# Macaron block (FFN, Mamba, FFN): other slots for the last two full iterations and an earlier preparation of the next group

## What is computed

```
x = x + 0.5 * ffn(layernorm(x))          # mixture of 8 experts, top 2, hidden 176 each, plus a shared FFN of 352
x = x + mamba(layernorm(x))              # 256 inner channels, 16 states, convolution of 4 taps, selective scan
x = x + 0.5 * ffn(layernorm(x))          # the same weights as the first
```

## Time and profile before

| what | value |
|---|---|
| median of 3 runs | 1891.11 us (1890.74 to 1896.28) |
| profiled execution, own time | 1897.91 us |
| span of its trace | 1896.2 us |
| mean granted TensorE clock in it | 0.956 |
| busy: PE, DVE, POOL, ACT | 1672.0, 1543.4, 1435.9, 1230.4 us |
| scans of iterations 12, 14, 15 begin at | 1404.26, 1618.79, 1713.01 us |
| last scan begins at | 1799.6 us |

### The profile page before, as it was taken

How to read it: one execution, slowest core, us unless ns; L and a number is a source line. 1 busy time by engine, 2 the same in 40 slices (tenths; PEclk the granted TensorE clock), 3 DMA queues, 4 the chain that set the end, 5 groups by cost and what they waited for, 6 DMA issues and landing times.

```text
span 1896.2 us, 27794 instructions
## 1 busy us (share of the span) xinstructions
PE 1672.0 (88%) x7378; PEld 1004.6 (53%) x7378; DVE 1543.4 (81%) x2337; ACT 1230.4 (65%) x1838; POOL 1435.9 (76%) x1318
## 2 busy tenths in 40 slices
PE   5888788989899998989989998999989898957488
PEld 3454444556565555556555555655555555634255
DVE  1358989899888988989888988989888998988732
ACT  2367677676858676676767676676766767665421
POOL 3346878878888887888888888788878888877753
PEclk9998799999999999999999999999999999979698
DMA  5127667686867778586777767677676868767742
GB/s 157 42 73 169 154 163 193 146 188 158 193 166 173 177 168 188 142 194 167 179 169 166 184 156 185 171 173 183 155 191 148 193 152 192 169 143 188 158 104 67
DMA packets 121344, 305.11 MB, mean 161 GB/s; under 512 B 19300, under 2 KB 40519, under 8 KB 106823
## 3 DMA queue, kind: packets, MB, share of 16 engines
q0 software_dynamic: 18432, 125.84, 33.5%
q1 hardware_dynamic: 98406, 174.46, 32.6%
q10 hardware_dynamic: 4320, 2.71, 0.5%
HBM read 167.67 MB, written 5.24 MB: 91 GB/s over the span
## 4 chain that ended last, share of the span: by engine, by line
PE 34%; DVE 19%; issue 15%; POOL 15%; ACT 8%; DMA 7%; DVEq 1%; ACTq 0%; SPq 0%; POOLq 0%
PE ps_y L1101 9%; DVE hist L927 7%; POOL prod L628 6%; PE ps_h2b L1109 5%; POOL gated L568 5%; PE ps_h1a L1087 5%; PE ps_h1b L1087 4%; DMA yacc<-prod 4%; PE ps_h2a L1109 3%; DVE ps_db L879 3%; DVE gated L907 2%; PE ps_m L1048 2%; ACT decay L691 2%; PE ps_m L1152 2%; DVE yacc L996 1%
## 5 line engine op out<-in xcount | busy, mean ns | idle before, releaser
L628 POOL TENSOR_TENSOR prod<-hist,crow 128x1024 f32<-128x1024 f32 x224 | 556.4, 2484 | 232.1 <-DVE hist L927 227.4
L1101 PEld LDWEIGHTS ps_y<-down_w,gated 128*128 128x128 f32 (+1 forms) x3584 | 471.8, 195 | 287.3 <-issue 156.2
L927 DVE TENSOR_TENSOR_SCAN hist<-decay,ps_db 128x1024 f32<-128x1024 f32 x256 | 583.2, 2278 | 2.8
L568 POOL TENSOR_TENSOR gated<-gated,silu 128x512 f32<-128x512 f32 x352 | 492.3, 1455 | 79.7 <-DVE gated L907 71.2
L1101 PE MATMUL ps_y<-down_w,gated 128*128 128x128 f32 (+1 forms) x3584 | 489.2, 281 | 68.2 <-POOL gated L568 67.1
L879 DVE TENSOR_TENSOR ps_db<-du,ps_db 128x1024 f32<-128x1024 f32 x256 | 313.0, 1222 | 103.9 <-PE ps_db L1069 101.2
L691 ACT ACTIVATE decay<-delta,a_neg 128x510 f32<-128x510 f32 x512 | 326.8, 708 | 5.7 <-DVE delta L970 4.3
L711 ACT ACTIVATE silu<-ps_h1a 128x512 f32<-128x512 f32 (+1 forms) x224 | 133.1, 594 | 257.2 <-PE ps_h1a L1087 256.5
L1087 PE MATMUL ps_h1a<-xnT,up_w 128*128 128x512 f32 (+1 forms) x448 | 238.7, 614 | 10.7 <-issue 10.7
L1087 PE MATMUL ps_h1b<-xnT,up_w 128*128 128x512 f32 x448 | 238.9, 615 | 5.2 <-ACT silu L711 4.7
L1109 PE MATMUL ps_h2b<-xnT,up_w 128*128 128x512 f32 x448 | 237.2, 612 | 1.7 <-DVE gated L907 1.7
(11 more groups left out here) (139 smaller groups left out, 1946.4 us busy)
## 6 DMA issues: line engine op xcount, KB each, us to landing
yacc<-prod POOLq DMA_DIRECT2D x112, 1024.0 KB, 10.0
crow<-c_rows SPq DMA_DIRECT2D x128, 512.0 KB, 5.0
wrow<-w_rows SPq DMA_DIRECT2D x320, 128.0 KB, 6.4
wrow<-w_rows SPq DMA_DIRECT2D x64, 224.0 KB, 7.0
wrow<-w_rows SPq DMA_DIRECT2D x64, 192.0 KB, 4.5
wrow<-w_rows SPq DMA_DIRECT2D x64, 160.0 KB, 3.0
yacc<-yacc POOLq DMA_DIRECT2D x16, 512.0 KB, 7.7
wrow<-w_rows SPq DMA_DIRECT2D x64, 96.0 KB, 3.2
```

Source lines behind the costliest of these rows:

```text
L568: nc.gpsimd.tensor_tensor(gated[:, pos % NGATE, :], gated[:, pos % NGATE, :], silu[:, (pos + NCHUNK * f_parity(of, f)) % NSILU, :], ALU.mu ...
L628: nc.gpsimd.tensor_tensor(prod[:, (pair - 1 + odd) % 2, s % 2, :, :], hist[:, s % 2, :, :], c_all, ALU.mult).then_inc(prod_done, 1)
L927: nc.vector.tensor_tensor_scan(hist[:, s % 2, :, :].rearrange("p h t -> p (h t)"), decay[:, s % NA, :, :, :].rearrange("p h b t -> p (h b ...
L1101: ins = nc.tensor.matmul(ps_y[:, t * C:(t + 1) * C], gated[0:rd, posd % NGATE, t * P:(t + 1) * P], down_w[0:rd, jd, :], start=(posd == 0 a ...
```

## The change

For iterations 14 and 15 there are tables of their own: END_UNIT puts the 14 chunks of the second FFN in slots 0, 2, 4 to 26, END_PLAN puts addy1 in slot 31 instead of 21, and END_SP has the row loads at later slots and store_x in slot 31, behind store_w1 and w1:0 to w1:3. Because chunks of the second FFN are now still read after slot 23, where xT1 writes the input of the next ones, xT1 writes xnT[0] in iterations 14 and 16 and xnT[1] in 15 (`second`); xnT[0] is free there.

In PLAN, which holds for the middle iterations and from which START_PLAN and END_PLAN are derived, dt0 and dt1 move from slots 17 and 18 to 14 and 15, sp_exp and xproj from 20 to 16, bparts from 22 to 16, sp_ln from 22 to 18, delta from 26 to 20, du from 28 to 22; in2 and in3 move from 14 and 15 to 19 and 21, wT0 from 16 to 17. The unit of slot 15 moves to 16. On SP store_w0 and w0:0 to w0:3 stand together in slot 18 (before 17 to 19).

```diff
@@ -54,20 +54,20 @@
     PLAN = {
         0: ["stats0"], 1: ["scale0"], 2: ["norm0"], 3: ["addy0", "fold"], 4: ["xT0"], 5: ["stats2", "scale2", "logits0"],
         6: ["norm2", "rcopy0"], 7: ["gate_y0", "xT2"], 8: ["gate_y1", "in0a"], 9: ["in0"], 10: ["outproj"],
-        11: ["resid", "route0"], 12: ["stats3", "in1a", "tilt0"], 13: ["in1", "scale3"], 14: ["in2", "ln_norm", "weights0"],
-        15: ["in3", "ln_scale"], 16: ["wT0", "ln_shift"], 17: ["dt0"], 18: ["dt1", "ln_add"], 19: ["stats1"],
-        20: ["sp_exp", "xproj", "scale1"], 21: ["addy1"], 22: ["norm1", "sp_ln", "bparts"], 23: ["xT1"], 24: ["logits1"],
-        25: ["rcopy1", "route1"], 26: ["cT", "delta"], 27: ["bT", "tilt1"], 28: ["weights1", "du"], 30: ["wT1"],
+        11: ["resid", "route0"], 12: ["stats3", "in1a", "tilt0"], 13: ["in1", "scale3"], 14: ["dt0", "ln_norm", "weights0"],
+        15: ["dt1", "ln_scale"], 16: ["sp_exp", "xproj", "bparts", "ln_shift"], 17: ["wT0"], 18: ["sp_ln", "ln_add"],
+        19: ["in2", "stats1"], 20: ["delta", "scale1"], 21: ["addy1", "in3"], 22: ["norm1", "du"], 23: ["xT1"],
+        24: ["logits1"], 25: ["rcopy1", "route1"], 26: ["cT"], 27: ["bT", "tilt1"], 28: ["weights1"], 30: ["wT1"],
     }
     EARLY = ("addy0", "addy1", "resid")
 
-    UNIT = {s: (1, pos) for pos, s in enumerate((0, 1, 2, 3, 4, 5, 6, 7, 8, 10, 12, 14, 15, 17))}
+    UNIT = {s: (1, pos) for pos, s in enumerate((0, 1, 2, 3, 4, 5, 6, 7, 8, 10, 12, 14, 16, 17))}
     UNIT.update({18 + pos: (0, pos) for pos in range(NCHUNK)})
     GATE, JOIN, BACK = 1, 2, 4
 
     SP_PLAN = {
         1: ["c1"], 3: ["c2"], 5: ["w1:4"], 6: ["w1:5"], 7: ["w1:6", "c3"], 8: ["w1:7"], 9: ["w1:8"], 10: ["w1:9"],
-        11: ["c4"], 12: ["w1:10"], 15: ["c5"], 17: ["store_w0", "w0:0", "w0:1"], 18: ["w0:2"], 19: ["c6", "w0:3"],
+        11: ["c4"], 12: ["w1:10"], 15: ["c5"], 18: ["store_w0", "w0:0", "w0:1", "w0:2", "w0:3"], 19: ["c6"],
         20: ["keep_x1n"], 22: ["store_x"], 23: ["w0:4", "c7"], 24: ["w0:5"], 25: ["w0:6"], 26: ["w0:7"], 27: ["w0:8"],
         28: ["w0:9", "next_c0"], 29: ["w0:10"], 31: ["store_w1", "w1:0", "w1:1", "w1:2", "w1:3"],
     }
@@ -90,14 +90,30 @@
         26: ["w0:9"], 28: ["w0:10", "next_c0"], 31: ["store_w1", "w1:0", "w1:1", "w1:2", "w1:3"],
     }
 
+    END_PLAN = {s: [n for n in names if n != "addy1"] for s, names in PLAN.items()}
+    END_PLAN[31] = ["addy1"]
+    END_UNIT = {2 * pos: (1, pos) for pos in range(NCHUNK)}
+    END_SP = {
+        1: ["c1"], 3: ["c2"], 7: ["c3"], 8: ["w1:4"], 10: ["w1:5"], 11: ["c4"], 12: ["w1:6"], 14: ["w1:7"], 15: ["c5"],
+        16: ["w1:8"], 18: ["w1:9"], 19: ["c6"], 20: ["w1:10", "keep_x1n"], 23: ["c7"], 28: ["next_c0"],
+        31: ["store_w1", "w1:0", "w1:1", "w1:2", "w1:3", "store_x"],
+    }
+
+    def end(k):
+        return isinstance(k, int) and G - 2 <= k < G
+
+    def second(k):
+
+        return 0 if isinstance(k, int) and k >= G - 2 and k % 2 == G % 2 else 1
+
     def start(k):
         return isinstance(k, int) and k < FULL
 
     def plan(k):
-        return START_PLAN if start(k) else PLAN
+        return START_PLAN if start(k) else END_PLAN if end(k) else PLAN
 
     def sp_plan(k):
-        return START_SP if start(k) else SP_PLAN
+        return START_SP if start(k) else END_SP if end(k) else SP_PLAN
 
     SETUP_MADE, SETUP_TAPS, SETUP_EDGE = 16, 24, 28
 
@@ -174,7 +190,7 @@
 
         back = slot < lag
         of, parity = (k - 1, 1 - odd) if back else (k, odd)
-        units = START_UNIT if start(of) else UNIT
+        units = START_UNIT if start(of) else END_UNIT if end(of) else UNIT
         if slot - lag + back * SLOTS not in units:
             return None
         f, pos = units[slot - lag + back * SLOTS]
@@ -713,7 +729,8 @@
                     for step in plan(k).get(slot, []):
                         if step == "xT0" and enters(k) or step == "xT1" and tail(k) or step == "xT2" and lead(k):
                             take(k, step)
-                            nc.scalar.activation(xnT[int(step[2])][:], ps_m[:], ACT.Copy).then_inc(misc_taken, 1)
+                            nc.scalar.activation(xnT[second(k) if step == "xT1" else int(step[2])][:], ps_m[:], ACT.Copy
+                                                 ).then_inc(misc_taken, 1)
                         elif step == "norm0" and enters(k):
                             plain_wait()
                             act.wait_ge(nbias_ready[0], k + 3)
@@ -1084,7 +1101,8 @@
                             pe.wait_ge(misc_taken, turn_last(k, "xT1") if f else turn(k, "xT0"))
                         if not isinstance(n, int) or n >= 2:
                             pe.wait_ge(silu_done, n - 1)
-                        nc.tensor.matmul(ps_h1[pos % 2][0:r, :], up_w[:, 0, j * P:j * P + r], xnT[f][:],
+                        xn_up = xnT[second(k - 1) if f else 0]
+                        nc.tensor.matmul(ps_h1[pos % 2][0:r, :], up_w[:, 0, j * P:j * P + r], xn_up[:],
                                          start=True, stop=True).then_inc(h1_full, 1)
                     d = unit(k, odd, slot, BACK)
                     if d is not None:
@@ -1106,7 +1124,7 @@
                     if u is not None:
                         if not isinstance(n, int) or n >= 2:
                             pe.wait_ge(h2_taken, n - 1)
-                        nc.tensor.matmul(ps_h2[pos % 2][0:r, :], up_w[:, 1, j * P:j * P + r], xnT[f][:],
+                        nc.tensor.matmul(ps_h2[pos % 2][0:r, :], up_w[:, 1, j * P:j * P + r], xn_up[:],
                                          start=True, stop=True).then_inc(h2_full, 1)
                     for step in plan(k).get(slot, []):
                         if step == "xT0" and enters(k) or step == "xT1" and tail(k) or step == "xT2" and lead(k):
@@ -1118,7 +1136,8 @@
                             f = int(step[6])
                             claim(k, step)
                             for t in range(TILES):
-                                ins = nc.tensor.matmul(ps_m[:, t * E:(t + 1) * E], xnT[f][:, t * P:(t + 1) * P],
+                                ins = nc.tensor.matmul(ps_m[:, t * E:(t + 1) * E],
+                                                       xnT[second(k) if f else 0][:, t * P:(t + 1) * P],
                                                        wg[:], start=True, stop=True)
                             ins.then_inc(misc_full, 1)
                         elif step == "wT0" and enters(k) or step == "wT1" and tail(k):
```

## The result

The changed kernel takes **1947.35 us** (median of four runs, 1945.41 to 1948.74) against 1891.89 us of the kernel before (four runs on the same chip, 1890.74 to 1896.28): ratio 1.028, 95% interval 1.026 to 1.030. It is slower; the forecast was 1860, and the range ended at 1892.

A forecast was written before the change was run, and what follows sets the result against it. PE was taken to lead, DVE close behind. 2.2 us in each of twelve middle iterations and 1 in each of the first two make 28; with 5 at the end, 33 us, forecast 1860, range 1838 to 1892.

The forecast's parts named there:

- What bounds the kernel: Middle iteration of 107.5 us: PE leads with 101.2 us of work, DVE close behind with 96.7; 6.3 us PE idle.
- Away from slots 22 to 31: Second half of middle iterations: DVE 4.3 to 6.0 us lighter, PE wins back 3.3 us of waits per iteration.
- 1.3 + 0.6: PE's waits on POOL's gated chunk: 1.3 of 2.34 us won back, 0.6 from two later waits counted half.
- brem and bparts in slot 16: wT0 at slot 17 waits for brem, with 1.7 us of PE matmuls between: 0 to 1.3 us lost, 0.3 taken.
- its scale of 1893: Whole kernel: the time without the change on the forecast's scale, the 1860 and the 33 us it wins.
- dt1 behind dt0: Slots 14 and 15: dt1 waits for ACT to empty the one PSUM tile, PE waits 1.4 to 1.6 us; net 1.0.
- the two halves: Middle iterations: 3.3 us gained away from slots 22 to 31, 1.1 lost into slots 14 to 20; balance 2.2.
- rival 1: Only the end gains: POOL sets the pace, middle 0, end 2 to 8 us, about 1885; chance 0.16.
- Rival 2: Gates of slots 22 to 24: router weights come late, kernel slower, 1909 with 17 us; chance 0.12.
- The end: Iterations 14 and 15: 6.3 + 1.6 us gained, 2.5 lost waiting for c1; 5 us, bounds -8 and 12.
- rival 3: Iterations 14 and 15: clock or c1 makes the end lose about 22 us; about 1887, or 1875; chance 0.12.
- The start: Iterations 0 and 1, with fewer units and looser engines, gain 1 us each; iteration -1 gains 0.

The follow-up runs named there:

- steps moved: Changed kernel with brem and md, the tail's drop and its hot each reading one operand from PSUM: 1871.55 us, ratio 0.988.
- unit back at slot 15: Changed kernel with the three reads from PSUM, unit of the thirteenth chunk back at slot 15 instead of 16: 1870.2 us, ratio 0.989.
- POOL's waits: Changed kernel, DVE untouched, two waits added on POOL: ln_shift waits for bparts, the product of slot 24 for the tail's hot: 1886.96 us, ratio 0.997.
- the last experiment: Kernel before with the end's tables, middle steps in old places, and three reads (brem and md, drop, hot) from PSUM: 1865.16 us, ratio 0.985, the fastest.

## Why the prediction was wrong

**What bounds the kernel: not contradicted.** In the four variants without the long shut-outs (steps moved, unit back at slot 15, steps in their old places, POOL's waits) the iteration settles at 107.2 to 107.8 us with PE busy 101.3 to 101.6 us and DVE 91.6 to 92.5. That PE sets the pace there was not tested by a run of its own.

**Away from slots 22 to 31: right for DVE, luck for PE's wait.** du took 1.20 us instead of 2.96. State 9 gained 2.4 us and state 11 2.1. PE's wait on the gated product fell by 22.9 us in total, 1.9 per iteration, which is the 1.3 + 0.6 that I had counted. But most of this fall came from PE standing elsewhere: once the shut-outs were gone, the same wait was back at 24.0 us with the steps moved, against 29.8 with the steps in their old places. That is 0.5 us per iteration, not 1.9.

**brem and bparts in slot 16: the step that failed.** The text priced brem's new place as "0 to 1.3 us, I take 0.3" of PE's wait, and the sum had no term for a brem longer than the one it had. It took 4.50 us, PE waited 3.3 us behind it, and the state grew by 5.3 us. The row was in front of me: brem ended with POOL's product. I read from it that a DVE instruction waits until the POOL instruction then at work ends. I never read POOL's timeline at the place to which brem was moved. There POOL goes from a DMA issue through ln_scale, gated, ln_shift and the product without a gap. The Trainium skill, page "SBUF — State Buffer", section "Who interferes with whom", says that whoever issues first has the shared port pair for the whole instruction, and that the other side blocks. This trace agrees on who interferes (the drop at 0.16 us with a PSUM operand, hot at 4.10 with none) and differs on how long: brem stood through the rest of the gated product and two further POOL instructions, drop through three further ones, though both had come before those began (brem 0.56 us, drop 0.08 us before the next one). The measurement decides. The range had no room for this either: even the sum's own bounds, -1 us in each of twelve iterations and -8 at the end, reach about 1913 on its scale of 1893, and the range stopped at 1892.

**The drop: a term that was missing.** route1 was not moved, so the sum had no entry for it. But steps that leave DVE ahead of it change what POOL does when it comes. Together the two states lost 8.8 us per iteration (5.3 and 3.5), the other states gained 5.0 net; the difference, 3.8, is what iterations 3 to 12 show.

**dt1 behind dt0: the wait right, its price not.** PE waited 1.4 us for dpre, as forecast (net 1.0). But with the unit back between the two the wait was gone and the time the same, so the 1.0 was not a loss of its own. That xproj, bparts and wT0 make state 8 longer even without a shut-out (5.84 to 7.25) I had at 0.3 us. With it the two halves cancel, as the last experiment shows: forecast +2.2 us per iteration, measured 0 with the same unit table as the change, 0.6 with the unit back. This is rival 1's outcome by another way: not POOL, but the slots that the steps were moved into, gave the gain back.

**Rival 2, late router weights: did not come.** DVE's wait on rows of wrow was 0.6 us in total between 240 and 1510 us. My "slower" case named the wrong mechanism. One small reading was off as well: "no table load is added" on ACT, where the trace has 290 table loads instead of 284.

**The end: about right in sum, and rival 3 partly came.** The tables gain about 3 us in iterations 14 and 15 against 5 forecast. State 0 of iteration 15 fell from 7.55 to 4.25 us and state 10 from 6.08 to 4.04, as priced. But the clock took part of it. The table by stretch of the changed kernel, states 2 to 5 of iteration 15:

```profile
1773.46:1777.50 4.04, 2.48 (x11) 1.19 (x10) 4.00 (x4) 4.01 (x6) 1.19 (x3) 1.00 0.97 255
1777.50:1785.09 7.59, 4.31 (x19) 2.15 (x18) 5.45 (x5) 5.33 (x8) 2.47 (x2) 0.99 0.73 190
1785.09:1790.52 5.43, 2.56 (x4) 0.90 (x5) 5.36 (x5) 2.38 (x3) 5.35 (x5) 0.50 0.36 95
1790.52:1798.86 8.34, 8.34 (x39) 5.88 (x40) 4.81 (x5) 0.84 (x2) 5.72 (x4) 0.72 0.99 228
```

PE, busy 2.5 of 4.0 and then 4.3 of 7.6 us, falls to a granted clock of 0.50 (1.2 GHz) in state 4. State 5 finds it at 0.72 and keeps PE busy for all of its 8.34 us. The out-projection has slipped from state 4 into state 5, so the two must be read together: 13.8 us here, 12.1 us before, when both ran at 1.00. That is 1.7 us lost (2.1 with the end's tables alone, state 5 at 0.68), though PE has fewer matmuls there (43 in the trace, 60 before): the two up-projections and the down-projection at the lower clock took 1.91, 1.92 and 2.08 us, where the same groups before took 1.02, 1.02 and 1.05. Ahead of the fall PE stood still, and behind that stands the row of C that SP now sends after the store. POOL, then PE:

```profile
1782.62 4.65 POOL L644 TENSOR_TENSOR prod<-hist,crow 128x1024 f32<-128x1024 f32 x2 [6.29 <-DMA crow<-c_rows]
...
1787.44 0.61 PE L1086 MATMUL ps_db<-bT,sel_b 96*128 96x512 bf16 x1 [4.59 <-DVE hist L944]
```

POOL waited 6.3 us for it, where the prediction had some 8. State 3, which ends with it, was no longer than before (7.60 and 7.75 us), but PE stood for 4.6 us. That this stop brought the clock down is likely and not shown, and what the wait cost in all was not measured by a run of its own. I had taken 1.00 for the states from 0 to 8; it held for states 1 to 3 and 6 to 8, with 0.62 in state 0. The Trainium skill, page "TensorE: Matmul & The Clock Gate", section "A second HAM failure mode: psum-queue depth-cycling", warns of such swings for a PE that pauses between its groups; the trace agrees in direction, at a small price. State 12 took another 3.3 us (6.72 to 10.04), where drop was held for 4.34 us as in the middle.

**The start.** Up to the scan of iteration 2 the changed kernel lost 10.4 us, for which the sum had a gain of 2. Where in the start it lies can't be read from one execution: the kernel before and the one with the end's tables alone have the same start, and their first scans are at 128.4 and 131.6 us, their scans of iteration 2 at 312.8 and 312.9. With brem from PSUM the latter is at 315.4 instead of 323.2, so most of this loss too is brem's.

What stays open: why POOL's instructions overlap after a DMA issue and not after a wait. And one such stop is still there in the fastest kernel: the gate step of the tail (yacc<-yacc,zs, two SBUF operands) took 2.72 instead of 0.69 us in 14 of its 32 cases there (15 in the kernel before), each beside a POOL product. Nobody tried the cure on it.

## What to carry to other kernels

Before a small VectorE instruction with two SBUF operands is moved, read GpSimd's timeline at its new place and at those of its neighbours: it can be held for as long as GpSimd's instructions overlap each other (here by 0.35 us; where the overlap was 0.05 us, VectorE got in between). One operand in PSUM, or one semaphore wait that opens a gap in GpSimd's run, removes that, and here such a wait stopped GpSimd for 0.8 to 1.0 us. When freeing one place gains less than its stall was long, look at what the states beside it now do, and try the same cure with the old order: here the cure with the end's tables was worth 1.5% and the move nothing.

## What the hardware showed unexpectedly

- A VectorE instruction of 0.16 to 0.22 us of work took 4.5 us (brem), 5.2 us (drop) and 4.1 us (hot), each until the end of GpSimd's run and not of one instruction.
- FIND_INDEX8 took 0.16 us in the middle of a GpSimd product; tensor_tensor on two SBUF tiles, 0.6 us later, was held for 4.1 us.
- GpSimd's gated product takes 1.27 us behind a wait and 1.55 to 1.6 us within a run that follows a DMA issue, where each begins 0.35 us before the one ahead ends.
